# Moving one addition of a graph-attention layer from VectorE to GpSimd, and VectorE's small pieces to earlier steps

## The reference

```python
def _gat_layer(x, W, adj):
    proj = x @ W
    Wh, Ws = jnp.split(proj, 2, axis=-1)
    scores = Wh @ Ws.T
    a = jax.nn.softmax(scores, axis=-1) * adj
    out = a @ Wh
    out = out + x
    return jax.nn.leaky_relu(out, NEG_SLOPE)
x = inputs
for l in range(W_stack.shape[0]):
    x = _gat_layer(x, W_stack[l], adj)
```

## Time and profile before

| | us |
|---|---|
| median of three runs | 473.91 |
| lowest and highest | 473.73, 473.94 |
| the profiled execution's own time | 474.03 |
| its span | 472.2 |
| TensorE matmuls busy | 461.6 (98%) |
| VectorE busy | 373.1 (79%) |
| ScalarE busy | 231.3 (49%) |
| GpSimd busy | 189.2 (40%) |

### The profile page before, as it was taken

How to read it: one execution, slowest core, us unless ns; L and a number is a source line. 1 busy time by engine, 2 the same in 40 slices (tenths; PEclk the granted TensorE clock), 3 DMA queues, 4 the chain that set the end, 5 groups by cost and what they waited for, 6 DMA issues and landing times.

```text
span 472.2 us, 5614 instructions
## 1 busy us (share of the span) xinstructions
PE 461.6 (98%) x1838; PEld 302.9 (64%) x1838; DVE 373.1 (79%) x830; ACT 231.3 (49%) x408; POOL 189.2 (40%) x186
## 2 busy tenths in 40 slices
PE   8999999999999999999999999999999999999993
PEld 7999755545555588787544444554557546778882
DVE  4688799999998689858137746999955697899984
ACT  6979529991888543333434532442333475342200
POOL 1444665631425036954001541452440073456641
PEclk9999999999999999999999999999999999999999
DMA  8856310001359100000000000000000000000001
GB/s 304 279 177 184 128 36 0 1 1 59 117 185 202 32 0 1 0 1 1 0 1 0 0 1 1 1 0 0 1 1 1 0 1 1 0 20 16 22 24 40
DMA packets 16500, 21.73 MB, mean 46 GB/s; under 512 B 9328, under 2 KB 13060, under 8 KB 16472
## 3 DMA queue, kind: packets, MB, share of 16 engines
q1 hardware_dynamic: 14648, 19.28, 13.2%
q10 hardware_dynamic: 1360, 1.31, 0.8%
q0 software_dynamic: 464, 0.79, 0.7%
HBM read 19.99 MB, written 1.39 MB: 45 GB/s over the span
## 4 chain that ended last, share of the span: by engine, by line
PE 75%; DVE 18%; issue 4%; DMA 1%; POOL 1%; ACT 0%; SPq 0%; POOLq 0%; DVEq 0%
PE psum L1590 16%; PE psum L1433 11%; PE psum L1394 11%; PE psum L1690 8%; PE psum L1375 6%; PE psum L1627 6%; PE psum L1570 3%; DVE ST L1082 3%; PE psum L1302 3%; PE psum L1542 2%; PE psum L1456 2%; PE psum L1661 2%; DVE rm L1031 2%; PE psum L1484 2%; DVE stats L782 1%
## 5 line engine op out<-in xcount | busy, mean ns | idle before, releaser
L1590 PE MATMUL psum<-QT,xT 128*128 128x512 f32 (+3 forms) x264 | 108.0, 542 | 0.0
L459 POOL TENSOR_TENSOR es<-es,ST 128x512 f32<-128x512 f32 (+3 forms) x60 | 75.9, 1265 | 55.2 <-ACT ST L658 53.5
L653 ACT ACTIVATE ST<-psum 128x512 f32<-128x512 f32 (+3 forms) x66 | 36.1, 546 | 91.6 <-DVE rm L1031 81.8
L1590 PEld LDWEIGHTS psum<-QT,xT 128*128 128x128 f32 (+1 forms) x264 | 48.2, 186 | 42.5 <-issue 35.9
L1031 DVE TENSOR_TENSOR rm<-psum,rm 128x512 f32<-128x512 f32 (+3 forms) x60 | 37.4, 623 | 40.6 <-PE psum L1590 40.4
L1690 PE MATMUL psum<-Wh,ST 128*128 128x256 f32 (+3 forms) x242 | 55.1, 380 | 0.0
L1627 PE MATMUL psum<-ST,Wh 128*128 128x512 f32 (+3 forms) x132 | 54.4, 543 | 0.6 <-DVE ST L1082 0.6
L386 POOL TENSOR_TENSOR rstd<-veps,nhalf 128x1 f32<-128x1 f32 (+1 forms) x44 | 29.2, 664 | 64.0 <-DVE veps L785 64.0
L414 POOL TENSOR_TENSOR esumb<-esumb,eb 128x1354 f32<-128x1354 f32 (+1 forms) x10 | 34.5, 3450 | 46.3 <-ACT eb L560 46.3
L1433 PE MATMUL psum<-eb,x_all 128*128 128x512 f32 (+3 forms) x132 | 51.9, 542 | 0.0
L1394 PE MATMUL psum<-adjT,x_all 128*128 128x512 f32 (+3 forms) x132 | 50.1, 542 | 0.0
(11 more groups left out here) (176 smaller groups left out, 775.0 us busy)
## 6 DMA issues: line engine op xcount, KB each, us to landing
adj_rows<-in_adj_dram SPq DMA_DIRECT2D x10, 677.0 KB, 5.5
rows<-in_adj_dram SPq DMA_DIRECT2D x10, 677.0 KB, 4.0
out_dram<-xs SPq DMA_DIRECT2D x10, 128.0 KB, 1.7
W<-in_L_gnn_W_stack_dram SPq DMA_DIRECT2D x2, 512.0 KB, 5.3
W3B<-in_L_gnn_W_stack_dram SPq DMA_DIRECT2D x8, 128.0 KB, 3.7
x_all<-in_x_dram ACTq DMA_DIRECT2D x3, 256.0 KB, 4.8
x_all<-in_x_dram SPq DMA_DIRECT2D x2, 256.0 KB, 5.2
adj_rows<-in_adj_dram SPq DMA_DIRECT2D x1, 338.5 KB
```

The lines of the kernel that those rows point to most:

```text
L459: nc.gpsimd.tensor_tensor(es[0:r, g % 2, 0:w], es[0:r, g % 2, 0:w], buf(g)[0:r, j, 0:w], ALU.add)\
L1590: last = nc.tensor.matmul(psum[0:r, SB[n % 3], 0:w], xT[l][:, k, j * P:j * P + r], QT[:, k, c0:c1], start=(k == 0), stop=(k == KD - 1))
```

## The change

GpSimd's queue gets one instruction, `add_input(0)`, behind addition 5 of chunk 1: it waits for the scaling of chunk 0 and adds the layer's input to it, which VectorE's `add_t(0)` did. On VectorE, `den_turn` of chunk 0 moves from behind step 1 to behind step 0, `den_gather` from 3 to 2, `den_spread` from 5 to 3 and `scale_t` from 6 to 4; `leaky_t` stays behind step 8. For chunk 1 the order is the same as before (scale behind step 0, add behind 1, leaky behind 2).

```diff
@@ -459,9 +459,17 @@
+            def add_input(g):
+
+                c0, c1, _ = chunk(g)
+                pool.wait_ge(gat_read.sem, g + 1)
+                nc.gpsimd.tensor_tensor(sums_of(g), sums_of(g), xT[0][:, :, c0:c1], ALU.add).then_inc(t_ready.sem, 1)
+
             for g in range(NC + 1):
                 for j in range(T):
                     add_probs(g, j)
+                    if (g, j) == (1, 5):
+                        add_input(0)
@@ -1189,7 +1197,7 @@
-            def turnover(g, last, add):
+            def turnover(g, last, scale):
@@ -1199,17 +1207,17 @@
                 for s in range(last):
                     both(g + 1, s)
-                    if g == 0 and s == 1:
+                    if g == 0 and s == 0:
                         den_turn(g)
+                    if g == 0 and s == 2:
+                        den_gather(g)
                     if g == 0 and s == 3:
-                        den_gather(g)
-                    if g == 0 and s == 5:
                         den_spread(g)
-                    if s == add - 1:
+                    if s == scale:
                         scale_t(g)
-                    if s == add:
+                    if g > 0 and s == scale + 1:
                         add_t(g)
-                    if s == add + 1:
+                    if s == (scale + 4 if g == 0 else scale + 2):
                         leaky_t(g)
@@ -1217,9 +1225,9 @@
-            turnover(0, T, 7)
+            turnover(0, T, 4)
             max_blocks(2)
-            turnover(1, CROSS, 1)
+            turnover(1, CROSS, 0)
```

## The result

| | before | after |
|---|---|---|
| median (18 runs each) | 473.80 us | 474.95 us |
| lowest to highest | 473.0 to 474.28 | 474.56 to 475.58 |
| ratio, 95% interval | | 1.0026 [1.0019, 1.0032] |
| span of the profiled execution | 472.2 | 473.8 |

The account below looks back on a forecast made before the run. TensorE bounds the kernel, with VectorE leading in this stretch, so its delays are paid nearly in full. Lost turns 6.33 - 3.83, less 1.14 of removed work, give 1.36, taken as 1.4: 473.9 + 1.4 = 475.3 us, range 474.8 to 475.8.

Parts of the forecast that it names:

- The new addition: GpSimd's addition of the input, 128x1024, behind the scaling: 2.36 us, with ends of 2.19 and 2.68.
- The lost turns: VectorE's waits for GpSimd in chunk 2's turnover(0): 6.33 us after the change against 3.83 before.
- Multiply 1 free and multiply 2 delayed: VectorE's early mask multiplies: the first finds GpSimd idle, 0.36 us saved; the second meets addition 3, 0.35 lost.
- spread: VectorE's spread copies, now behind step 3: addition 5 gets in behind the first copy, 1.06 us lost.
- multiply 5: VectorE's mask multiply of step 5: waits 1.38 us for the turn while GpSimd's new addition runs.
- multiplies 6 to 8: VectorE in lockstep with GpSimd's late additions: rounds of 1.85 us against 1.61, 0.24 more for each.
- multiply 9: VectorE's mask multiply of step 9: a lost turn of 0.66 us, as before the change.
- leaky's turn: VectorE's leaky behind step 8: late addition 9 is ahead of it, 1.08 us lost where nothing was before.
- TensorE's waits: TensorE late by 0.65 us at the score tile, 1.5 at multiply 5's sum, 1.4 at multiply 9's; the last decides.
- The copies: Rival: addition 5 does not slip between the spread's copies, 1.06 us is not paid; 474.2 us, chance 0.14.
- The longer hold: Rival: the new addition takes 2.68 us and late GpSimd meets one copy more next turnover; 475.9 us, chance 0.08.
- The turn was lost: Its rival: GpSimd's new addition costs multiply 5 no turn and delays no additions; 473.0 us, chance 0.08.

Follow-up runs that it names:

- e4: The changed kernel with GpSimd's addition of the input behind addition 8 instead of 5; ratio to the kernel before the change 1.0015.
- e5: The changed kernel with the spread right behind the gather in step 2, where GpSimd is idle; ratio to the kernel before the change 1.0017.
- e6: The changed kernel with GpSimd's addition of the input replaced by a fill of about the same duration; ratio to the kernel before the change 1.0032.
- e9: The kernel before the change with only GpSimd's addition of the input, behind addition 6, VectorE's pieces in their old places; ratio 1.0054 to the kernel before.
- e10: The kernel before the change with only GpSimd's addition of the input, behind addition 7, run again for a second profile; ratio 1.0033 to the kernel before.
- e3: The changed kernel with the addition of the input left out for chunk 0 of the first layer; ratio to the kernel before the change 0.9996.
- e7: The kernel before the change with the seven small copies of chunk 0's gather and spread on ScalarE; ratio to the kernel before 0.9988.
- e8: The changed kernel with the seven small copies on ScalarE and VectorE's spread moved to step 4; ratio to the kernel before the change 0.9980.
- e2: The kernel before the change with only GpSimd's addition of the input, behind addition 7, VectorE's pieces in their old places; ratio 1.0032 to the kernel before.

## Why the prediction was right

- **The forecast.** 475.3 us against 474.95, and a shift of 1.4 against 1.2 [0.9 to 1.5] in the runs and 1.39 in the profile. A part of the gap of 0.35 is the base: I counted from 473.91, the median of three runs, where 18 runs give 473.80.
- **What bounds it.** Right, in both directions. A delay of VectorE came through in full (exit and mark are equal in the change, e4, e5, e6, e9 and e10), and a gain was cut: e3's 0.70 and e7's 3.62 gave 0.17 and 0.98. The most that a gain could be was 0.87 by my count and 0.98 in e7 and e8. The 0.11 between them is in the rows: behind its wait the sum of 321.65 took 323.48 - 321.65 = 1.83 to the next start, where a sum without a wait takes 1.72, and I had counted the waits alone.
- **The new addition.** 2.36 taken from the line between two widths, 2.36 in the profile.
- **The lost turns.** Multiply 1 free and multiply 2 delayed (1.03 in the profile), gather 1.76 for four copies as before, spread 1.06 (addition 5 in behind the first copy, as told), multiply 5 2.06 - 0.68 = 1.38, multiplies 6 to 8 0.25 each (1.86 apart in place of the 1.85 told), leaky 2.29 - 1.21 = 1.08, multiply 9 0.67. Each is within 0.02 of its term. The sum was 1.36 and the exit moved by 1.39. One cause was told too simply: I put leaky's turn down to the late additions, but e3, with none of them late, loses it too. The term is right for this order, and e3 shows that the new addition did not bring it.
- **TensorE's waits.** By the starts the score tile is 0.74 late (306.54 + 1.72 is 308.26, it began at 309.00; 0.65 told). The sum that needs multiply 5 began 313.75 - 294.94 = 18.81 into the stretch and 312.04 - 294.77 = 17.27 before, 1.54 late (1.5 told). Multiply 9 ends 1.39 later than before (1.4 told). The wait for it is hidden in a merged row: 319.50 plus 3.44 is 322.94, and the projection behind the third sum began at 325.03, less the 1.83 of a sum behind a wait 323.20, so that sum waited about 0.26, a size that I had not told.
- **The rivals.** The copies did not get by, and e5, which takes them out of GpSimd's way, is 0.58 over before (that case was priced at 0.3), since multiply 4 then loses a turn. The longer hold did not come. The turn was lost, and e3 shows what the case without it would have given: TensorE's mark 0.17 earlier, not 0.87. The moved spread holds TensorE up near 308 by 0.74, and by 0.08 more for its first matmul behind the wait, which the rival's price had left out: 0.98 less 0.82 is 0.16. VectorE would have left 0.70 earlier, not 0.95. That price was wrong; the forecast's own sum does not use it.

The row behind TensorE's first wait in the kernel before, for the 1.83:

```profile
323.48 3.60 PE L1570 MATMUL psum<-xT,M 128*128 128x512 f32 x8
```

## What to carry to other kernels

Before moving an elementwise operation from VectorE to GpSimd, look at what both do around it: here instructions of VectorE with two SBUF inputs and its SBUF copies took turns with GpSimd's reads of SBUF, so VectorE gave up 1.14 us of work and lost 2.5 us more in turns. If GpSimd's queue feeds the same engine, the instructions behind the new one are late too, and taking away only the turn or only a part of the lateness gives little back. The small copies between such instructions were better given to ScalarE, where they took 0.22 us each beside a GpSimd addition that kept its 1.27 (e7): that gave all that TensorE's waits had to give, 0.98 us at its mark. And before any of it, add up the bound engine's waits in the stretch: some 0.9 to 1 us was the most that any such edit could win.

## What the runs showed of the hardware that I had not expected

A wait of TensorE of 1.87 us was followed in one profile of three (e2, its repeat e10, and e9) by a granted clock of 0.71 and 0.86 over 8 us, and cost 1.3 us more; in the other two, with waits of 1.85 and 1.90, by nothing. Over all runs of these kernels 4 of 16 show the lower mean clock, against 1 of 158 of the others. The two costs of a long GpSimd instruction, the turn it holds and the lateness behind it, overlap: of 2.09 us, the removal of the one gave back 0.38, and of a part of the other 0.53. And a fill on GpSimd held no turn: a multiply issued within its 2.44 us kept 0.68. The Trainium skill (SBUF — State Buffer, Who interferes with whom) says this of instructions that only write SBUF; e6 agrees.
